# Storing and loading softmax maxima from ScalarE's DMA queue instead of SyncE's

## The reference

```python
x = xn @ W_qkv + b_qkv
q, k, v = jnp.split(x.reshape(B, 16, S, -1), 3, axis=-1)
qk = jnp.einsum('bhse,bhte->bhst', q, k) * scale
attn = softmax(qk + causal_mask)
sa = jnp.einsum('bhst,bhte->bhse', attn, v)
out = input + (sa @ W_out + b_out) + light_ffn(xn) + heavy_ffn(selected rows of xn)
```

## Time and profile before

| | |
|---|---|
| median of three runs | 706.35 us (704.91 to 706.52) |
| profiled execution, first to last instruction (the only time given of it) | 705.6 us |
| PE busy | 660.3 us, 94% |
| DVE busy | 563.1 us, 80% |
| ACT busy | 392.4 us, 56% |
| POOL busy | 380.6 us, 54% |
| bytes moved by DMA | 92.48 MB in 259776 packets |

### The profile page before, as it was taken

The page is one execution under the profiler, slowest core; times in us unless marked ns, Lnnn a source line. Parts: engine busy times, 40 slices in busy tenths (PEclk is TensorE's granted clock), DMA queues, the critical chain, the costliest instruction groups (busy, mean ns, idle before and its releaser), DMA issues. The chain is left out here.

```text
span 705.6 us, 12334 instructions
## 1 busy us (share of the span) xinstructions
PE 660.3 (94%) x3923; PEld 291.7 (41%) x3923; DVE 563.1 (80%) x1587; ACT 392.4 (56%) x876; POOL 380.6 (54%) x774
## 2 busy tenths in 40 slices
PE   4995999899999999989999999999999999999995
PEld 2552555333333333323323333333333434678675
DVE  4853888899999999999999999999999595563211
ACT  2331322387877777728858868777776565230210
POOL 4663550358858657657886755554543274431603
PEclk9997999899999999979999999999999999999999
DMA  8675999769786676795999648458484261956512
GB/s 274 195 183 159 230 237 235 173 134 153 136 140 138 90 139 103 97 145 94 164 152 150 122 87 120 74 54 118 79 159 35 42 123 34 207 107 163 106 60 30
DMA packets 259776, 92.48 MB, mean 131 GB/s; under 512 B 229808, under 2 KB 245328, under 8 KB 256592
## 3 DMA queue, kind: packets, MB, share of 16 engines
q1 hardware_dynamic: 258176, 89.60, 65.9%
q0 software_dynamic: 1536, 2.10, 1.7%
HBM read 56.65 MB, written 35.01 MB: 130 GB/s over the span
## 5 line engine op out<-in xcount | busy, mean ns | idle before, releaser
L1268 DVE CUSTOM_DVE_ANT_0 ps<-ps,maskrow 128x640 f32<-128x640 f32 (+7 forms) x512 | 375.3, 779 | 27.6 <-PE ps L1034 26.0
L904 ACT ACTIVATE strips<-ps 128x512 f32<-128x512 f32 (+1 forms) x608 | 313.0, 577 | 111.0 <-PE ps L1076 88.7
L1034 PE MATMUL ps<-QTk,QTq 96*128 96x512 bf16 (+3 forms) x768 | 190.5, 337 | 22.6 <-DVE mx L1268 15.4
L1076 PE MATMUL ps<-QTq,QTk 99*128 99x512 bf16 (+3 forms) x768 | 185.4, 331 | 1.5 <-DMA QTq<-m_d 0.6
L1094 PE MATMUL ps<-strips,vext 128*32 128x512 f32 (+3 forms) x1536 | 162.0, 497 | 0.9 <-DVE oT L1291 0.4
L1034 PEld LDWEIGHTS ps<-QTk,QTq 96*128 96x128 bf16 x768 | 53.7, 98 | 170.9 <-DVE mx L1268 137.2
L1076 PEld LDWEIGHTS ps<-QTq,QTk 99*128 99x128 bf16 x768 | 68.4, 98 | 88.3 <-ACT strips L904 40.2
L1747 POOL TENSOR_SCALAR_AFFINE_SELECT strips<-strips 128x512 f32<-128x512 f32 x128 | 79.4, 636 | 41.6 <-ACT strips L904 41.2
L994 PE MATMUL ps<-shared,xrT 128*128 128x384 f32 (+1 forms) x256 | 94.9, 503 | 0.1
L1268 DVE DVE_READ_ACCUMULATOR2_ANT mx<- 128x1 f32 x512 | 72.3, 141 | 0.0
L1640 POOL TENSOR_TENSOR r<-qkT,pieces 128x1024 f32<-128x1024 f32 x16 | 34.1, 2132 | 50.2 <-ACT pieces L883 41.9
(11 more groups left out here) (154 smaller groups left out, 668.3 us busy)
## 6 DMA issues: line engine op xcount, KB each, us to landing
pieces_d<-pieces SPq DMA_DIRECT2D x64, 192.0 KB, 3.5
qk<-qkv_d SPq DMA_DIRECT2D x64, 128.0 KB, 3.9
qkv_d<-shared SPq DMA_DIRECT2D x16, 384.0 KB, 4.0
QTq<-pieces_d SPq DMA_DIRECT2D x16, 384.0 KB, 5.1
QTk<-pieces_d SPq DMA_DIRECT2D x16, 384.0 KB, 7.6
QTq<-pieces_d SPq DMA_DIRECT2D x16, 256.0 KB, 5.7
QTk<-pieces_d SPq DMA_DIRECT2D x16, 256.0 KB, 8.3
vext<-qkv_d SPq DMA_DIRECT2D x16, 256.0 KB, 5.8
```

The costliest lines, as they stand in the source:

```text
L904: nc.scalar.activation(dst, src, ACT.Exp, scale=SCALE).then_inc(exp_done, 1)
L1034: mm = pe.matmul(psM[:, s, at:at + n], QTq[0:W, f % 3, c * 1024 + qb * P:c * 1024 + (qb + 1) * P], QTk[0:W, f % 3, c * 1024 + k0:c * 1024 ...
L1076: mm = pe.matmul(psE[:, (NE * q + j) % ES, k * n:(k + 1) * n], QTk[0:W + 3, q % 3, c * 1024 + kb * P:c * 1024 + (kb + 1) * P], QTq[0:W + 3 ...
L1268: ins = nc.vector.tensor_tensor_reduce(scores, scores, maskrow[:, 1024 - n:1024], 1.0, MASKED, ALU.add, ALU.max, mx[:, f % 2, 8 * c + qb:8 ...
```

## The change

The store of the maxima becomes one transfer of all 128 partitions, 192 bytes each, into a tensor laid out like `mP`. The load becomes three transfers, one for each of the three rows of `QTq`, which gather 128 pieces of 64 bytes. Both are issued by ScalarE, between its exponentials, with the waits that SyncE had: for GpSimd's four steps, for the store to land, and for the ring's buffer to be free. Block 0's pair is issued at the end of ScalarE's front loop, before the table load. The semaphore `m_in` becomes three, one for each buffer of the ring. In the planner, MW and LM move from SyncE's list to ScalarE's, with the costs 0.45 and 1.0, and land LANDS + 0.4 after their issue.

```diff
-SCALAR = {"P1": 1.1, "RX": 0.5, "R": 0.25}
+SCALAR = {"P1": 1.1, "RX": 0.5, "R": 0.25, "MW": 0.45, "LM": 1.0}
-SYNC = {..., "MW": 1.7, "LM": 0.3, ...}        MOVES = {..., "MW": 0.2, "LM": 0.3, ...}
+SYNC = {...}                                   MOVES = {...}
...
-        ("Sync", "LM"): [x for f in range(1, STEPS) for x in (("MW", f), ("LM", f))],
+        ("Scalar", "LM"): [x for f in range(1, STEPS) for x in (("MW", f), ("LM", f))],
...
+            if kind == "MW":
+                return after(("Pool", ("MAX", x[1])))
+            if kind == "LM":
+                return latest(done.get(("landed", ("MW", x[1]))), 0.0 if x[1] < 3 else after(("Tensor", ("E", x[1] - 3, NE - 1))))
...
+        if x[0] in ("MW", "LM"):
+            done["landed", x] = end + LANDS + 0.4
...
-        m_d = nc.dram_tensor("m_d", [NQ, 3, 4096], BF16).ap()
+        m_d = nc.dram_tensor("m_d", [NQ, P, 3, 32], BF16).ap()
...
-        m_in = sem("m_in")
+        m_in = [sem(f"m_in{b}") for b in range(3)]
...
-            def store_m(f):
-                sp.wait_ge(max_done, 4 * f + 4)
-                rows = m_d[f].rearrange("i (n g j) -> g n i j", g=4, j=32)
-                for g in range(4):
-                    sp.dma_start(rows[g], mP[32 * g:32 * g + 32, :, :]).then_inc(m_st, 16)
-            def load_m(f):
-                sp.wait_ge(m_st, 64 * (f + 1))
-                if f >= 3:
-                    sp.wait_ge(qk_ps, NE * (f - 2))
-                sp.dma_start(QTq[W:W + 3, f % 3, :], m_d[f]).then_inc(m_in, 16)
...
-                elif t == FIRST_DONE + 3:
-                    store_m(0)
-                elif t == FIRST_DONE + 4:
-                    load_m(0)
...
+            def store_m(f):
+                act.wait_ge(max_done, 4 * f + 4)
+                act.dma_start(m_d[f], mP[:, :, :]).then_inc(m_st, 16)
+            def load_m(f):
+                act.wait_ge(m_st, 16 * (f + 1))
+                if f >= 3:
+                    act.wait_ge(qk_ps, NE * (f - 2))
+                for i in range(3):
+                    act.dma_start(QTq[W + i:W + i + 1, f % 3, :].rearrange("i (n g j) -> i n g j", g=4, j=32),
+                                  m_d[f].rearrange("(g n) i j -> i n g j", g=4)[i:i + 1]).then_inc(m_in[f % 3], 16)
+            store_m(0)
+            load_m(0)
...
-                    pe.wait_ge(m_in, 16 * (q + 1))
+                    pe.wait_ge(m_in[q % 3], 48 * (q // 3 + 1))
...
-                    pool.wait_ge(m_st, 64 * f)
+                    pool.wait_ge(m_st, 16 * f)
```

More of the change, by code:

```diff
@@ L83 @@
 VECTOR = {"TP": 1.17, "MXT": 0.15, "OT": 0.65, "OREC": 0.18, "R": 0.36, "S": 0.8, "ST": 0.2, "SMAX": 1.2, "L": 0.67, "KEY": 0.9, "TIES": 1.2, "SLOTS": 0.5, "HOT": 0.95, "N": 0.4}
-SCALAR = {"P1": 1.1, "RX": 0.5, "R": 0.25}
+SCALAR = {"P1": 1.1, "RX": 0.5, "R": 0.25, "MW": 0.45, "LM": 1.0}
 GPSIMD = {"SPLIT": 5.5, "MAX": 1.2, "CAUSAL": 0.68, "RA": 1.6, "S": 2.9, "ROUTES": 1.8, "SA": 0.65, "NA": 0.3, "CX": 2.5, "G": 2.1}
-SYNC = {"LQK": 2.2, "LV": 0.6, "STORE": 2.2, "LOAD": 1.6, "MW": 1.7, "LM": 0.3, "SA": 2.4, "S_OUT": 0.5, "S_IN": 2.5, "NA_OUT": 0.5, "NA_IN": 0.5, "XC": 2.0, "BULK": 4.0}
-MOVES = {"LQK": 3.6, "LV": 2.8, "STORE": 3.4, "LOAD": 4.6, "MW": 0.2, "LM": 0.3, "SA": 2.8, "S_OUT": 0.3, "S_IN": 1.5, "NA_OUT": 0.3, "NA_IN": 0.3, "XC": 6.0, "BULK": 9.0}
+SYNC = {"LQK": 2.2, "LV": 0.6, "STORE": 2.2, "LOAD": 1.6, "SA": 2.4, "S_OUT": 0.5, "S_IN": 2.5, "NA_OUT": 0.5, "NA_IN": 0.5, "XC": 2.0, "BULK": 4.0}
+MOVES = {"LQK": 3.6, "LV": 2.8, "STORE": 3.4, "LOAD": 4.6, "SA": 2.8, "S_OUT": 0.3, "S_IN": 1.5, "NA_OUT": 0.3, "NA_IN": 0.3, "XC": 6.0, "BULK": 9.0}
 LANDS = 1.6
@@ L258, in ready @@
                           0.0 if x[1] < 3 else after(("Tensor", ("E", x[1] - 3, NE - 1))))
[L259 to L262, removed]
         if kind == "SA":
@@ L807, in _ @@
                     load_pieces(item[1], item[2])
[L808 to L811, removed]
                 elif item[0] == "SA":
@@ L920, in _ @@
                     first_piece(item[1])
+                elif item[0] == "MW":
+                    store_m(item[1])
+                elif item[0] == "LM":
+                    load_m(item[1])
                 elif item[0] == "RX":
```

## The result

The changed kernel takes 724.17 us in the median of four runs (723.12 to 726.32) beside 706.43 us (704.91 to 707.99) for the kernel before: a ratio of 1.0242, interval 1.0216 to 1.0268. It is some 17 us slower; the forecast, 706.4 us, and its range, 702 to 711.5 us, are both missed. The profiled execution's span went from 705.6 us to

What follows compares the result with a forecast made beforehand. VectorE was taken to set the middle stage's pace, TensorE at its heels; 705.6 - 1.0 (hole) - 0.4 (end) + 1.5 (pauses) = 705.7 us, with 0.75 us around it 706.4 us; range 702 to 711.5 us.

Steps and rivals of the forecast that it cites:

- The landing of 2.2 us: Each load of 64-byte pieces was taken to land in 2.2 us, as block 15's load has now.
- the wait of TensorE for the maxima: TensorE waiting for a load of the maxima: 0.6 us in the run before, in two places; no added wait forecast.
- The second rival: Slower: small pieces land late, 5.8 us instead of 2.2, TensorE stands at blocks' first scores; 10 us, 716 us; chance 0.05.
- The order: Planner's order written anew on every engine; closing block 6's 14.2 us hole in TensorE's scores gives back about 1.0 us.
- The cover of 2.3 us: Middle stage: VectorE's two full slots, 2 x 1.17 us of work, hide ScalarE pauses up to about 2.3 us.
- The price of a load: Issue of each of a block's three loads on ScalarE, taken as 0.33 us between bounds 0.252 and 0.87 us.
- The wait for the store: ScalarE waiting before the loads until the store lands: 0.45 us at the longest landing seen, inside the 2.3 us.
- SyncE's relief: SyncE loses 1.97 us of issue a block and its waits; worth at most 0.6 us, mostly nothing.
- block 0: Its store and loads, 2.9 us, fit ScalarE's 7.78 us idle stretch until 132.20 us at the front loop's end; zero cost.
- The first rival: Slower: ScalarE's pauses, three loads of 0.87 us in a row, outlast VectorE's two slots; 4.5 us, 710.9 us; chance 0.25.
- the upper bound of this part: ScalarE's pauses at worst: store and three loads in one piece, 3.47 us, 1.2 us over cover, 15 times, 18 us.
- the signs named ahead: Forecast right: VectorE's waits 10 to 18 us, no ScalarE pause past 2.3 us; many blocks' TensorE waits would show slower rivals.

Runs made afterwards that it cites:

- e6: Changed planner's new order without the transfers: only block 0's maxima go through memory and all blocks read them; 707.84 us, ratio 1.0013 to the kernel before.
- e2: Changed kernel's order and ScalarE queue with the old shapes, four stores and one load of three rows; 721.23 us, ratio 1.0193 to the kernel before.
- e4: The changed kernel's new order, with the old four stores and one load on SyncE's queue; 720.26 us, ratio 1.0204 to the kernel before.
- e8: Kernel before, in its own order, with the new shapes (one store, three loads) issued by SyncE; 708.04 us, ratio 1.0002.
- e1: Changed kernel; SyncE holds back a block's operand loads until the maxima of two blocks earlier have landed; 715.06 us, ratio 1.0109 to the kernel before.
- e9: Kernel before plus three idle transfers in a row on ScalarE in each block, which nothing waits for; 711.73 us, ratio 1.0082.
- e7: Kernel before plus five idle transfers in a row on ScalarE in each block, which nothing waits for; 727.47 us, ratio 1.0286.
- e3: Order of the kernel before; only the transfers, in their new shapes (one store, three loads), stand on ScalarE; 718.08 us, ratio 1.0144.
- e5: Kernel before, in its own order, without the maxima's stores and loads for blocks 1 to 15; all blocks read block 0's maxima; 707.57 us, ratio 0.9999.
- e15: Order of the kernel before, new transfers on ScalarE, SyncE's operand loads held back until the maxima of two blocks earlier landed; 718.32 us, ratio 1.0166.
- e10: Kernel before plus five idle transfers per block on ScalarE, put singly, 3.6 us apart in the planned order; 708.71 us, ratio 1.0022.

## Why the prediction was wrong

**The landing of 2.2 us is the step that failed, and with it the wait of TensorE for the maxima that I put at nothing.** The 2.2 us are right in the median and wrong where it counted: in blocks 7 and 8 loads landed after up to 8.1 and 6.9 us, TensorE stood 6.5 and 4.5 us, and VectorE's waits there grew by 14.5 us (against e6), nearly the whole loss. Two readings led there. I took the 3.1 us "at most" of the earlier trace rows for loads too, and it holds stores alone; and one landing, block 15's, at a time without SyncE's bulk loads, stood for all. The second rival, to which I gave 0.05, had the effect and the wrong cause. It isn't the size of the pieces: loads of three whole rows are late as well, read 5.7 us after issue in e2 and in e4. So the rule of the Trainium skill (DMA: Bandwidth & Descriptors, Specifications) doesn't show as a cost here: e8, with the small pieces in the old order, runs at 1.0002. The loads land late where SyncE's qk and operand loads go out beside them; holding the operand loads back brings the longest landing of a load to 4.1 us and at least 9.4 us of time back (e1).

**The order** was given -1.0 us for a closed hole. The hole did close (block 6's first score comes 8.6 us earlier), and e6 shows that by itself the new order is worth nothing that can be told, 1.0013. What the estimate lacked is that a closed hole is lost slack: block 7's load had 9.9 us until it was read before, and 3.0 us in the new order, where every late landing is a stop. e4 shows that this order loses 2.0% with the transfers on SyncE as well.

**The cover of 2.3 us** failed too, though the changed kernel's loss doesn't come from it. "The point from which pauses cost is thus about 2.3 us" rested on the 1.06 us copy and VectorE's two full slots. In the old order e9 measured 5.8 us for stops of 1.25 us, e7 20 us for stops of 2.4 us: the price rises by degrees, from well under the point that I named. One reason is shown: VectorE waits not for scores alone but for ScalarE's row sums, past all slots (4.8 us in e7, 4.3 us in e3). Another is only argued: the copy has its place in the planned order, and the issue comes on top of it (e7's lines have the two side by side). The changed kernel fits that: its order has places for the transfers, and its stops left no mark outside blocks 7 to 9.

**The price of a load was half.** I took 0.33 us "nearer the load" of the earlier trace rows; it is 0.62 us, near the middle of the bounds 0.252 and 0.87 us. A block costs 0.34 + 3 x 0.62 = 2.2 us instead of 1.43 us. The shape sets it, not the queue: 0.60 us on SyncE (e8). The store I had at 0.43 us; it takes 0.34.

**The wait for the store** was put at up to 0.45 us. In block 2 ScalarE stood 183.55 - 182.02 = 1.5 us for it.

**Right** were the zeros: SyncE's relief (e5, 0.9999), though its 42.5 us of waiting for the maxima did vanish from its page, the shapes (e8), and block 0, whose store and loads lie between 123.1 and 127.9 us in front of a first copy at 132.56 us. The first rival, slower by pauses, has its mechanism in the old order (e3, e7, e15), and gave 4.5 us where e3 lost 10; in the changed kernel no run shows a share of it. I had 18 us as the upper bound of this part and let the range end at the rival's 4.5 us; with the bound in it, it would have reached 724 us, about the result, by luck, for the loss came from the loads. Of the signs named ahead, VectorE's waits (27.1 us against 10 to 18), the stops over 2.3 us and TensorE's wait for the maxima (in two blocks, not in many) all spoke for the slower rivals; block 6 without a hole came with them, not with a gain.

## What to carry to other kernels

Before a new order closes an idle stretch, ask which transfer's late landing that stretch was hiding, and take a landing from a row in which the same other loads go out beside it, not from the median. When both the order and the queue change, run each without the other, and the new order without the transfers: the last shows block by block where the loss sits.

An engine with 26% of idle time isn't free to issue transfers that its order does not provide for: five in a row stopped ScalarE for 2.4 us in the median, and stops of one or two microseconds cost this kernel, whose two other engines are full. Put a transfer on a computing engine singly behind a long instruction and where it doesn't have to wait for a landing, and follow every engine that reads from the stopped one, small steps too.

## What the runs showed of the hardware

An issue of 0.50 us on ScalarE ran beside an exponential of 0.49 us and left no gap behind it (e10); of five in a row, 3.1 us of issue, 2.1 to 3.5 us were left as a stop (e7). A load of 128 pieces of 64 bytes into one partition takes a median of 0.55 to 0.62 us of issue on ScalarE and 0.60 us on SyncE, a load of three whole rows 0.25 us on either (e2). Three such loads of pieces land in 2.2 us in the median; beside SyncE's qk and operand loads they take up to 8.1 us on ScalarE's queue, and up to 8.2 us on SyncE's own (e8). Loads of whole rows are late there as well, read 5.7 us after their issue on either queue (e2, e4). After TensorE's stop of 6.5 us the granted clock was 0.56 over the next 7 us, with the engine busy throughout.
